# Graph network on one core: one unread 16-bit product of 384 columns before each transposition of edge features

## The chip, the cores and the metric

The kernel runs on one core of a Trainium2 chip. The metric is the device time of one execution in microseconds (us). The core has TensorE (PE; its weight loads are listed as PEld), VectorE (DVE), ScalarE (ACT), GpSimd (POOL) and SyncE (SP), which only issues transfers here. A measurement of this kernel can tell a change of about 0.2% (8 us) from no change.

## What is computed

Four layers of a graph network over 3125 nodes with 128 features and 103125 directed edges (50000 drawn pairs in both directions, and one loop per node), each of the form "normalise, clip at zero, layer, add to x". Cut to what matters here:

```python
h = jnp.maximum(_layernorm(x, axis=-1), 0.0)
# layer 0: a message per edge, summed by source node
msg_input = concatenate([h[dst], edge_attr_64], axis=1)
m = leaky_relu(msg_input @ msg_w1 + msg_b1) @ msg_w2 + msg_b2
aggregated = segment_sum(m, src)
x = x + leaky_relu(concatenate([h, aggregated]) @ upd_w1 + upd_b1) @ upd_w2 + upd_b2
# layer 1: attention with a weight per edge type; layers 2 and 3: sums over the same edges
```

The stage that the change touches makes, for every edge, the row `edge_attr_64 @ msg_w1[128:]` and puts it at the edge's place in a list that is sorted by pairs of node tiles.

## The kernel before

The nodes lie in 25 tiles of 128, so that an edge falls into one of 625 bins (tile of src, tile of dst). A first stage counts the edges of each bin. The second, called the scatter here, is the one that is changed. Later stages go through the sorted rows, build matrices of counts, and do the layers as dense products.

The edges lie 806 to a partition ("columns" of 128 edges). A body of the scatter's loop handles 26 columns in two halves of 13 (`CH`), and there are 31 bodies (62 halves). In one body:

- SP loads the 64 features of the edges of a half into `ef` (L639 to L644) when TensorE has turned the last pair that lay in that half's buffer (`s_te`).
- TensorE goes through 13 pairs of columns (`step`, L838). For a pair q it turns two columns at once (L844, a 32-bit transposition of 128 columns into `pe_t[:, q % 2, 0:P]`), which ACT copies to `eT` (L703); the pair before is then multiplied with `w1bb` (L836, 32 bits, 256 columns, carried out in two passes that the trace lists separately) and ACT copies the result into `rows` (L687). For q equal to 0 and `MEET` (6) the product L836 stands ahead of the transposition. `pe_t` has two banks of 512 words a partition, of which a transposition uses the first 128 words.
- Between the pairs TensorE also works for the half after next: it turns one-hot matrices (L805), spreads the bins over the partitions (L813, 16-bit products of 128 columns) and looks up where a bin begins (L826).
- VectorE works out each edge's place: 13 sums `junkR` (L761), the look-up (L766 to L771), then, for the half after, the one-hots (L731 to L740) and 13 sums `junkW` of the relation's weight (L745), and only then the place as an integer, `posi` (L754).
- POOL sends each column with an indirect transfer to its places in `sorted_rows` in HBM (L885), 26 in a body. Ahead of the first column of a half it waits for `posi` and for the indices, and ahead of the first, fifth and ninth column for `s_cq`, the count of pairs that ACT has copied into `rows` (`NEED`: 2, 4 and 7 pairs in the first half, 9, 11 and 13 in the second).
- ACT fills the index columns of a half (L696, L698) only when the scatters that last read this half of `rows` have landed and VectorE's sums L745 are there.

So the queue that a reader should follow is POOL's: nothing else in the stage reaches `sorted_rows`, and the next stage starts when the last transfer has landed.

Of the kernel before, what the change touches and what calls it, by code (L numbers as in the profile page):

```python
# [22 lines left out]
P = 128  # L23
# [53 lines left out]
def build(nc, x, src, dst, ea, et, w1, b1, w2, b2, u1, c1, u2, c2,  # L77
# [6 lines left out]
    with ExitStack() as top:  # L84
# [102 lines left out]
        with ExitStack() as srt:  # L187
            def sb(name, shape, dt=F32):
                return srt.enter_context(nc.sbuf_tensor(name, shape, dt))
# [10 lines left out]
            identh = sb("identh", [P, P], F16)  # L200
# [365 lines left out]
            with ExitStack() as ctx:  # L566
# [3 lines left out]
                def pb2(name, shape, dt=F32):  # L570
                    return ctx.enter_context(nc.psum_tensor(name, shape, dt))
# [26 lines left out]
                pe_t = pb2("s_pet", [P, 2, BANK])  # L598
# [31 lines left out]
                def prev(i, q):  # L630
                    return (i, q - 1) if q else (i - 1, PAIRS - 1)

                def after(i, h):
                    return (i, 1) if h == 0 else (i + 1, 0)
# [162 lines left out]
                def _(pe):  # L797
                    def turn(i, h, first):
                        n = i * 2 + h
                        pe.wait_ge(s_hv, n + 1)  # L800
                        if not first:
                            pe.wait_ge(s_ot, n)
                        for q in range(4):
                            a, b = 4 * q, min(4 * q + 4, CH)
                            last = nc.tensor.transpose(tq[0:(b - a) * QP, q, :], ohF[:, h, a:b, :].rearrange("p c s -> p (c s)"), identh[:])  # L805
                        last.then_inc(s_tt, 1)

                    def bin_rows(i, h, g, first):
                        n = i * 2 + h
                        if not (first and g < 2):  # L810
                            pe.wait_ge(s_rk, n * 4 + g - 1)
                        for c in range(4 * g, min(4 * g + 4, CH)):
                            last = nc.tensor.matmul(br[:, g % 2, c % 4, :], binh[:, h, c:c + 1].to_broadcast([P, P]), identh[:],  # L813
                                                    start=True, stop=True)
                        last.then_inc(s_br, 1)

                    def lookups(i, h, part, first):
                        n = i * 2 + h
                        if part == 0:
                            pe.wait_ge(s_ot, n + 1)  # L820
                            if not first:
                                pe.wait_ge(s_lc, 3 * n - 2)
                        for q in PARTS[part]:
                            a, b = 4 * q, min(4 * q + 4, CH)
                            k = (b - a) * QP
                            last = nc.tensor.matmul(lk[:, a * NT:b * NT], ohT[0:k, h, q, :],  # L826
                                                    base[0:k, h, q, 0:b - a, :].rearrange("p j d -> p (j d)"), start=True, stop=True)
                        if part == 2:
                            last.then_inc(s_lk, 1)

                    def project(i, q, first):
                        n = i * PAIRS + q
                        pe.wait_ge(s_ce, n + 1)
                        if not (first and q < 2):
                            pe.wait_ge(s_cq, n if q == 0 else n - 1)
                        nc.tensor.matmul(pe_q[:, q % 2, 0:2 * D], eT[:, q % 2, :], w1bb[:], start=True, stop=True).then_inc(s_q, 1)  # L836

                    def step(i, first, final):  # L838
                        for q in range(PAIRS):
                            if q in (0, MEET):  # L840
                                pe.wait_ge(s_row[q // MEET], i * 48 + 48)
                                if not (first and q == 0):
                                    project(*prev(i, q), first)
                            nc.tensor.matmul(pe_t[:, q % 2, 0:P], efv[:, 2 * q * ED:2 * (q + 1) * ED], ident[:], is_transpose=True,  # L844
                                             start=True, stop=True).then_inc(s_te, 1)
                            if q not in (0, MEET):
                                project(*prev(i, q), first)
                            h, r = (0, q) if q < MEET else (1, q - MEET)
                            if not (final and h):
                                to = after(i, h)  # L850
                                if r == 1:
                                    turn(*to, False)
                                if r in (1, 2, 3, 4):
                                    bin_rows(*to, r - 1, False)
                                if r == 5:
                                    for part in range(3):
                                        lookups(*to, part, False)
# [1204 lines left out]
```

## Time and profile before

| | us |
|---|---|
| median of 3 runs | 4012.09 |
| the runs | 4009.74, 4012.09, 4016.07 |
| the profiled execution | 4007.71 |
| its span | 4006.0 |

| engine | busy us | share of the span |
|---|---|---|
| PE | 2767.3 | 69% |
| DVE | 2620.8 | 65% |
| POOL | 1983.2 | 50% |
| ACT | 1608.0 | 40% |

Shares of a whole span are means over stages with different limits. The scatter takes the time from about 278 us to about 1545 us. A row of the timeline gives start, duration, engine, line, operation and tiles, and in square brackets the idle time of the engine before it and what ended that. "issue" is a wait for nothing that the profile shows, "remote" one for a semaphore whose last update the profile can't lay to an instruction. The granted clock is the share of 2.4 GHz that TensorE got; it has two levels, 1.2 and 2.4 GHz.

### The profile page before, as it was taken

What the parts mean: (1) busy time and instruction counts of PE and PEld (TensorE: products, weight loads), DVE (VectorE), ACT (ScalarE), POOL (GpSimd) and SP (SyncE); (2) the same over time, 40 slices, a digit from 0 to 9 for tenths busy, and PEclk for the clock granted to TensorE, in tenths of its full rate; (3) what the DMA queues carried; (4) which work ended last, traced back from release to release, by engine and by line L of the source; (5) the groups of instructions that cost most, each with busy time, mean ns of one, the idle gap of its engine ahead of it and who ended that gap; (6) DMA issues with size and microseconds to landing.
All of it is one profiled execution on the core that took longest, in us unless ns stands there. A gap on an engine that the chain in (4) does not pass through costs nothing. (4 is left out here: it accounts for less than half of the span.)

```text
span 4006.0 us, 89562 instructions
## 1 busy us (share of the span) xinstructions
PE 2767.3 (69%) x19674; PEld 2009.0 (50%) x19675; DVE 2620.8 (65%) x7923; ACT 1608.0 (40%) x4084; POOL 1983.2 (50%) x2354
## 2 busy tenths in 40 slices
PE   2314554455454555888888888888888967769599
PEld 2213333333333334787777877787785222234345
DVE  8724555555555554888888888888886759950501
ACT  1001222222222223776777777776775613320201
POOL 0015666566666666777777777777772000000100
PEclk9955556666666657999999999999999979979797
DMA  9971222221222223777777777777774848848082
GB/s 387 415 291 59 65 65 63 64 62 61 64 64 65 65 64 106 205 203 202 204 204 203 202 206 202 202 205 197 202 206 171 294 173 295 296 151 325 22 325 100
DMA packets 702415, 696.60 MB, mean 174 GB/s; under 512 B 51182, under 2 KB 633536, under 8 KB 692640
## 3 DMA queue, kind: packets, MB, share of 16 engines
q1 hardware_dynamic: 672706, 637.13, 50.5%
q0 software_dynamic: 25792, 54.52, 4.0%
q10 hardware_dynamic: 3870, 4.37, 0.3%
q8 instruction: 24, 0.39, 0.0%
q14 instruction: 23, 0.19, 0.0%
HBM read 340.91 MB, written 354.90 MB: 174 GB/s over the span
## 5 line engine op out<-in xcount | busy, mean ns | idle before, releaser
L885 POOL DMA_INDIRECT sorted_rows<-rows,posi x806 | 779.8, 967 | 577.1 <-issue 246.4
L836 PE MATMUL s_peq<-sb_w1bb,eT 128*128 128x256 f32 x806 | 395.5, 591 | 584.9 <-ACT eT L703 359.6
L1166 DVE SCALAR_TENSOR_TENSOR acc<-acc,keep,pm 128x256 f32<-128x256 f32 x1504 | 717.4, 477 | 76.3 <-DVE acc L1166 36.3
L997 POOL TENSOR_SCALAR ohs_e<-iota,rt 128x128 f32<-128x128 f32 x1128 | 669.6, 608 | 11.4 <-DMA rt<-sorted_rows 11.4
L1093 PE MATMUL pm<-ohw_e,ohs_e 128*128 128x128 f32 x3008 | 662.7, 302 | 0.0
L1006 POOL TENSOR_TENSOR hid<-pre_e,excess 128x512 f32<-128x512 f32 x376 | 498.7, 1326 | 313.5 <-ACT excess L1033 313.5
L836 PEld LDWEIGHTS s_peq<-sb_w1bb,eT 128*128 128x128 f32 x806 | 188.9, 288 | 635.3 <-ACT eT L703 398.7
L1099 PE MATMUL px<-PN,dT 128*128 x4512 | 498.5, 219 | 0.2 <-ACT dT L1040 0.2
L1049 ACT ACTIVATE ohw_e<-ohd_e,rt 128x128 f32<-128x128 bf16 x1504 | 474.6, 386 | 0.0
L1092 PE MATMUL pm<-ohd_e,ohs_e 128*128 128x128 bf16 x1504 | 334.3, 222 | 198.1 <-DVE acc L1166 182.8
L1093 PEld LDWEIGHTS pm<-ohw_e,ohs_e 128*128 128x128 f32 x3008 | 459.7, 193 | 0.0
L703 ACT ACTIVATE eT<-s_pet 128x128 f32<-128x128 f32 x403 | 110.2, 274 | 773.0 <-remote 521.8
L1110 PE MATMUL ps<-hid,ohs_e 128*128 128x129 f32 x3008 | 417.9, 281 | 1.5 <-POOL hid L1006 1.5
L1033 ACT ACTIVATE excess<-pre_e 128x512 f32<-128x512 f32 x376 | 237.0, 630 | 420.3 <-DVE pre_e L1154 420.3
L1099 PEld LDWEIGHTS px<-PN,dT 128*128 128x128 bf16 x4512 | 382.8, 99 | 18.5 <-issue 0.5
L1110 PEld LDWEIGHTS ps<-hid,ohs_e 128*128 128x128 f32 x3008 | 365.5, 191 | 2.1 <-POOL hid L1006 1.9
L1978 POOL TENSOR_TENSOR Z<-Z,Q 128x640 f32<-128x640 f32 x5 | 9.1, 1825 | 712.5 <-DVE Q L1956 712.5
L745 DVE SCALAR_TENSOR_TENSOR junkW<-iotar,typc,relt 128x100 f32<-128x100 f32 x806 | 218.7, 319 | 169.5 <-issue 166.9
L1146 DVE TENSOR_TENSOR ohd_e<-iota,rt 128x512 bf16<-128x512 bf16 x376 | 265.0, 705 | 83.0 <-DMA rt<-sorted_rows 74.2
L1850 PE MATMUL num<-ab,hw 128*128 128x512 f32 (+1 forms) x700 | 274.4, 555 | 18.8 <-DMA ab<-count_matrices 18.8
L1092 PEld LDWEIGHTS pm<-ohd_e,ohs_e 128*128 128x128 bf16 x1504 | 146.2, 97 | 277.8 <-DVE acc L1166 245.3
L761 DVE SCALAR_TENSOR_TENSOR junkR<-s_binrows,binc,later 128x128 f32<-128x128 f32 x806 | 226.5, 345 | 71.5 <-remote 32.6
(299 smaller groups left out, 4469.3 us busy)
## 6 DMA issues: line engine op xcount, KB each, us to landing
count_matrices<-acc SPq DMA_DIRECT2D x1504, 128.0 KB, 2.0
ab<-count_matrices SPq DMA_DIRECT2D x75, 1600.0 KB, 7.8
sorted_rows<-zrow SPq DMA_DIRECT2D x188, 528.0 KB, 9.9
rt<-sorted_rows SPq DMA_DIRECT2D x376, 264.0 KB, 3.0
arb<-count_matrices SPq DMA_DIRECT2D x25, 1664.0 KB, 6.8
arb<-count_matrices SPq DMA_DIRECT2D x25, 1536.0 KB, 6.4
ef<-in_edge_attr_dram SPq DMA_DIRECT2D x60, 364.0 KB
sorted_rows<-rows,posi POOLq DMA_INDIRECT x806
```

Of the source, the lines that this page charges most:

```text
L836: nc.tensor.matmul(pe_q[:, q % 2, 0:2 * D], eT[:, q % 2, :], w1bb[:], start=True, stop=True).then_inc(s_q, 1)
L885: pool.indirect_dma_start(sortd, bass.IndirectOffsetOnAxis(ap=posi[:, h, c:c + 1], axis=0), rows[:, h, c, :], None).then_inc(s_sc[h], 16)
L997: last = nc.gpsimd.tensor_scalar(ohs[:, k, j, :], iota128[:], rt[:, k, j, D + 1:D + 2], None, ALU.is_equal)
L1006: nc.gpsimd.tensor_tensor(hid[:, k % 2, :, 0:D], pre[:, k % 2, :, :], excess[:, k % 2, :, :], ALU.add).then_inc(s_g, 1)
L1049: last = nc.scalar.activation(ohw[:, k, j, :], ohd[:, k, j, :], ACT.Copy, scale=rt[:, k, j, D + 2:D + 3])
L1092: nc.tensor.matmul(pm[:, q, j % 2, 0:P], ohs16[:, kp, j, :], ohd[:, kp, j, :], start=True, stop=True)
L1093: last = nc.tensor.matmul(pm[:, q, j % 2, P:2 * P], ohs[:, kp, j, :], ohw[:, kp, j, :], start=True, stop=True)
L1099: last = nc.tensor.matmul(px[:, kh % 2, j, :], dT[:, kh % 2, j, :], PN[:, ds(dt[j], 1), part, :].squeeze(1), start=(part == 0), stop=(part ...
L1110: last = nc.tensor.matmul(ps[:, k % 2, 0:D + 1], ohs[:, k, j, :], hid[:, k % 2, j, :], start=(j == 0), stop=(j == G - 1))
L1146: nc.vector.tensor_tensor(ohd[:, k, :, :], iota16[:].unsqueeze(1).to_broadcast([P, G, P]), rt[:, k, :, D:D + 1].to_broadcast([P, G, P]), A ...
L1166: nc.vector.scalar_tensor_tensor(acc[:, k % 2, j, :], before, keep[:, at:at + 1] if isinstance(at, int) else keep[:, ds(at, 1)], pm[:, j / ...
L1850: last = nc.tensor.matmul(num[:, c, 0:b - a], hw[:, r, :], ab[:, r, :, :].rearrange("p q d -> p (q d)")[:, a:b], start=first and r == 0, s ...
```

## The change

One matrix product is added ahead of each transposition L844, 403 times in all (13 in a body): the 16-bit identity `identh` as the weights, and the identity again, read three times over, as the moving operand of 384 columns. It writes columns 128 to 511 of the bank of `pe_t` whose first 128 columns the transposition writes. Nobody reads them, and the product signals nothing and waits for nothing of its own. For q equal to 0 and `MEET` it stands behind the product L836 of the pair before, otherwise ahead of it.

```diff
@@ -841,6 +841,8 @@
                                 pe.wait_ge(s_row[q // MEET], i * 48 + 48)
                                 if not (first and q == 0):
                                     project(*prev(i, q), first)
+                            nc.tensor.matmul(pe_t[:, q % 2, P:4 * P].rearrange("p (a b) -> p a b", a=3), identh[:],
+                                             identh[:].unsqueeze(1).to_broadcast([P, 3, P]), start=True, stop=True)
                             nc.tensor.matmul(pe_t[:, q % 2, 0:P], efv[:, 2 * q * ED:2 * (q + 1) * ED], ident[:], is_transpose=True,
                                              start=True, stop=True).then_inc(s_te, 1)
                             if q not in (0, MEET):
```

## Rows read from the trace of the kernel before

**Rows 1.** The page, the span in 40 slices: TensorE's granted clock in tenths

```profile
PEclk9955556666666657999999999999999979979797
```

**Rows 2.** Busy time by stretch: the stage, then two bodies; clock, DMA share, GB/s last

```profile
278.00:1545.00 1267.00, 631.51 (x2647) 433.18 (x2647) 640.48 (x3801) 272.68 (x1019) 779.78 (x806) 0.62 0.20 63
1097.94:1139.41 41.47, 22.31 (x91) 15.85 (x90) 22.11 (x131) 9.04 (x34) 25.22 (x27) 0.58 0.20 63
1139.41:1179.14 39.73, 19.43 (x91) 13.23 (x91) 21.78 (x133) 9.05 (x34) 25.30 (x26) 0.67 0.21 66
```

**Rows 3.** The page's groups: busy, mean ns of one, idle before and its releaser

```profile
L885 POOL DMA_INDIRECT sorted_rows<-rows,posi x806 | 779.8, 967 | 577.1 <-issue 246.4
L745 DVE SCALAR_TENSOR_TENSOR junkW<-iotar,typc,relt 128x100 f32<-128x100 f32 x806 | 218.7, 319 | 169.5 <-issue 166.9
```

**Rows 4.** Waits of POOL, 278 to 1545 us: total, times, longest

```profile
POOL sorted_rows L885 <- ACT rows L687: 238.0, 61, 7.5
```

**Rows 5.** Timeline of POOL: first and last scatter, and the pauses of two bodies

```profile
278.05 1.20 POOL L885 DMA_INDIRECT sorted_rows<-rows,posi  x1 [92.74 <-DMA sorted_rows<-zrow]
...
1097.94 0.95 POOL L885 DMA_INDIRECT sorted_rows<-rows,posi  x1 [3.62 <-ACT rows L687]
...
1108.10 0.96 POOL L885 DMA_INDIRECT sorted_rows<-rows,posi  x1 [0.30 <-issue]
...
1113.82 0.95 POOL L885 DMA_INDIRECT sorted_rows<-rows,posi  x1 [0.30 <-issue]
1119.45 0.95 POOL L885 DMA_INDIRECT sorted_rows<-rows,posi  x1 [4.67 <-ACT rows L687]
...
1134.86 0.96 POOL L885 DMA_INDIRECT sorted_rows<-rows,posi  x1 [0.30 <-issue]
1139.41 0.96 POOL L885 DMA_INDIRECT sorted_rows<-rows,posi  x1 [3.59 <-ACT rows L687]
...
1152.07 0.96 POOL L885 DMA_INDIRECT sorted_rows<-rows,posi  x1 [2.81 <-ACT rows L687]
...
1179.14 0.96 POOL L885 DMA_INDIRECT sorted_rows<-rows,posi  x1 [4.31 <-ACT rows L687]
...
1541.28 0.96 POOL L885 DMA_INDIRECT sorted_rows<-rows,posi  x1 [0.30 <-issue]
```

**Rows 6.** Timeline of PE behind a pause, at the lower clock

```profile
1116.99 1.22 PE L836 MATMUL s_peq<-sb_w1bb,eT 128*128 128x256 f32 x2 [7.36 <-ACT eT L703]
1118.00 0.63 PE L813 MATMUL s_binrows<-identh,binh 128*128 128x128 f16 x4
...
1119.50 0.31 PE L813 MATMUL s_binrows<-identh,binh 128*128 128x128 f16 x1
...
1120.67 1.99 PE L826 MATMUL s_looked<-base,ohT 128*128 128x100 f32 x8
1122.59 0.47 PE L844 MATMUL s_pet<-ident,ef 128*128 128x128 f32 x1
```

**Rows 7.** Timeline of PE, at the higher clock

```profile
1151.47 0.70 PE L836 MATMUL s_peq<-sb_w1bb,eT 128*128 128x256 f32 x2 [0.88 <-ACT eT L703]
1152.91 0.40 PE L813 MATMUL s_binrows<-identh,binh 128*128 128x128 f16 x4 [0.73 <-DVE junkR L761]
...
1153.99 0.23 PE L813 MATMUL s_binrows<-identh,binh 128*128 128x128 f16 x1
```

**Rows 8.** Timeline of ACT: the seventh pair's copy, and the restart at a pause

```profile
1105.83 0.38 ACT L687 ACTIVATE rows<-s_peq 128x256 f32<-128x256 f32 x1 [1.23 <-PE s_peq L836]
1116.66 0.28 ACT L703 ACTIVATE eT<-s_pet 128x128 f32<-128x128 f32 x1 [10.45 <-remote]
...
1118.25 0.39 ACT L687 ACTIVATE rows<-s_peq 128x256 f32<-128x256 f32 x1 [0.37 <-PE s_peq L836]
```

**Rows 9.** Timeline of DVE: the last weight sum of a half and the place

```profile
1136.62 0.32 DVE L745 SCALAR_TENSOR_TENSOR junkW<-iotar,typc,relt 128x100 f32<-128x100 f32 x1 [1.32 <-issue]
...
1138.02 0.17 DVE L754 CAST posi<-posf 128x13 int32<-128x13 f32 x1 [0.60 <-issue]
```

## The prediction

> **What bounds the kernel now.** The slices come first: TensorE's clock stands at five or six tenths from slice 3 to slice 15 and near nine tenths behind them [rows 1]. That stretch is the scatter, the only stage that the change touches; over it TensorE is busy half of the time at a granted clock of 0.62, so a mix of 1.2 and 2.4 GHz [rows 2]. The engine groups then say who is the queue there: POOL issues 806 scatters of 967 ns with 0.30 us between two of them, 1.26 us a column [rows 3, 5]. Twenty-six columns would take 32.8 us, but from the first scatter at 278.05 to the end of the last at 1542.24 a body takes 1264.2 / 31 = 40.78 us. The missing 8 us are pauses: POOL waited 61 times, 238.0 us in all, for ACT's copies of projected pairs, about once a half [rows 4].
>
> The timeline shows what a pause is. POOL's last scatter of a half ends at 1114.77; ACT, idle for 10.45 us although its input was turned long before, goes on at 1116.66, 1.9 us behind that end [rows 5, 8]. At the next pause the last scatter ends at 1135.82, and VectorE, whose sums had crept with gaps of 1.3 us, goes on at 1138.02, 2.2 us behind it [rows 5, 9]. While POOL scatters without a break the other engines all but stop after a few columns; about 2 us after POOL itself pauses they are let go. I call that the release. I can't say from the rows what holds them, only that what ends it is tied to POOL's own stop. So most of a pause is 2 us of release plus what POOL then still needs: in the first half about 1.4 us; in the second the chain copy, product L836 of 1.22 us, copy at 1118.25, then 0.8 us until POOL's scatter at 1119.45 [rows 5, 6, 8].
>
> Not all bodies pause alike. The one from 1097.94 pauses twice at a half's border, 4.67 and 3.59 us (0.3 us of it is the usual gap), and takes 41.47 us. The one from 1139.41 pauses 2.81 us ahead of the ninth column of its first half (at 1152.07), crosses the next border without a pause, pauses 4.31 us at the one after, and takes 39.73 us [rows 2, 5]. An inner pause brings the release earlier and spares one at the border: 1.74 us less. From the mean of 40.78, the share of bodies of the second kind is (41.47 - 40.78) / 1.74 = 0.40.
>
> **The change part by part.** It removes nothing, moves nothing in a queue and adds no wait and no signal; 403 products of 384 columns and their weight loads are put into TensorE's queue. Price of one: four 16-bit products of 128 columns take 0.63 us and one takes 0.31, so each further 128 columns cost 0.107 us at the lower clock; at the higher one (0.40 - 0.23) / 3 = 0.057 [rows 6, 7]. Thus 384 columns cost 0.32 or 0.17 us; the weight load runs beside the product ahead of it, as that of L813 does, which I take as nothing (0.1 us each if that cover fails). In total 403 x 0.32 = 129 us, or 69 us at the higher clock, on an engine that is idle half of the stage.
>
> Where do they lie? TensorE is held for 7.36 us before each restart [rows 6]; what it may run ahead in that time costs nothing. Behind the release it works without a gap at the lower clock, from 1116.99 through look-ups that end at 1122.66 to a transposition at 1122.59 [rows 6]. In this run stand two products ahead of the look-ups (0.64 us), three ahead of the transposition that lets SP load the next features (0.96 us), and a fourth ahead of the seventh pair's L836 (1.28 us, or 0.7 if all were at the higher clock). Who waits for it: VectorE for the look-ups, POOL at its ninth column for the seventh pair. POOL's border pauses themselves start later than any of that and are ended by the release, and the L836 in the chain behind it has no added product in front that could not run earlier.
>
> The ninth column first. In the body from 1097.94 the seventh pair's copy ends at 1106.21, POOL could go 0.8 us later, at 1107.0, and went at 1108.10 [rows 5, 8]. The slack is 1.1 us, the added delay 0.7 to 1.28 us, most of it at the lower clock. So POOL will now often pause ahead of the ninth column where it just didn't before. That is no loss of its own: such a pause makes the release earlier, and the body gets the shorter kind. I take the share of that kind from 0.40 to 0.70, as the delay about equals the slack: 31 x 0.30 x 1.74 = 16 us less. In the remaining 0.30 of bodies I put 0.2 us for a pause too short to release anybody: 2 us more. Sum: 14 us less. Between the ends: share 1.0 gives 31 x 0.6 x 1.74 = 32 us less, and an unchanged share with the whole 1.28 us handed on in each of 62 halves gives 79 us more.
>
> The profiled execution took 4007.71 us (span 4006.0 and 1.7 around it), 4.4 us under the median of 4012.09. The forecast is 3994 for a profiled one, 3998 for the median.
>
> A rule of the Trainium skill speaks for more. What the rows show: the clock is at the lower level right behind each stretch of 7 to 10 us in which TensorE had nothing to do [rows 6], and at the higher one near 1152 after several microseconds of work [rows 7]. "TensorE: Matmul & The Clock Gate", Part 1, says that the throttled clock is the default and that activity releases it. The added products are activity, though none falls into the idle stretches, since they hang in the same queue behind the same waits.
>
> **The rivals.** First, slower: the products lie on a chain that is not forgiven. VectorE's last sum of the half ends at 1136.94 and `posi` follows at 1138.02, the time of the release [rows 9]: a margin of at most 1.1 us, against 0.64 us that the look-ups, and so the thirteen sums, come later, on an engine that at that time creeps with gaps of 1.3 us. From the point at which the delay costs one such step more than the margin, one or two sums are left behind the release, each 0.25 to 0.32 us [rows 3], and POOL's place waits for them: some 0.4 us a half, 62 x 0.4 = 25 us more, 4037. For it speaks that margin and delay are of one size; against it that in the same moment ACT's and TensorE's chain is as long, and covers some of it. Second, no change: the release is tied to POOL's stop, the 16 us of a half's thirteen scatters hide all of TensorE's 2 us more, and the inner pauses come from something other than the pairs' lateness, since the 2.81 us at 1152.07 stand in a body whose pairs were stopped, not slow. Then 4012 within 8. Third, the clock: if TensorE kept 2.4 GHz through the pauses, its L836 behind the release would take 0.70 us in place of 1.22 [rows 6, 7], some 0.45 us of every second pause: 31 x 0.45 = 14 us less, 3998 by another way; with the first term it would be 3984. By the skill's rule this could come; against it stand the idle stretches, which stay. Last, the change may not do what it is made of: if the granted clock of the stage stays at 0.62, TensorE has only got more work, and the first two rivals and the forecast are all that is left; this is how I read it, with 3 in 4.
>
> **How the numbers follow.** The forecast (more inner pauses, 3998) gets 0.38, slower by the delay 0.31, no change 0.23, the clock 0.08. Faster by over 0.2% (8 us, what a measurement can tell) is the forecast and the clock less what of them falls inside 8 us, 0.44; slower 0.32; within 0.24. As both signs hold much, the likeliest case's own range is 3980 to 4004; the range for 8 in 10 goes from 3974 (all bodies of the short kind, and something from the clock) to 4040 (the rival's 25 us and 3 more).
>
> **What would show it.** Right: about as many border pauses fewer as there are pauses ahead of the ninth column more, POOL's total wait for ACT near 225 us in place of 238.0, a clock near 0.65, the stage shorter by 14 us and every stage behind it as long as before. The delay step is right if the look-ups end 6.3 us behind the restart in place of 5.7. Wrong: if `posi` comes later than ACT's copies at the pauses, the first rival holds; if TensorE's first product behind a pause takes 0.70 us, the third. It would also be wrong if the hold on the engines depended on how much TensorE issues: then it would set in earlier, and no row of before can price that.

## The result and the profile after

The change makes the kernel slower. The median went from 4011.09 us (4002.29 to 4018.15, 14 runs) to 4027.32 us (4018.05 to 4035.48, 14 runs), a ratio of 1.0037 with an interval of 1.0025 to 1.0048: 16 us more, where 14 us less were forecast. That lies inside the widest range given (3974 to 4040), on the side of the first two rivals.

The page of the kernel after gives TensorE's clock in 40 slices and the group of POOL's scatters (busy, mean ns of one, idle before them and what ended most of it):

```profile
PEclk9956676666666667999999999999998979979797
L887 POOL DMA_INDIRECT sorted_rows<-rows,posi x806 | 779.2, 967 | 576.0 <-ACT rows L687 242.0
```

Within the stage one slice stands at five tenths, where five did before [rows 1]. The scatters cost what they did [rows 3]. Over the stage, busy time by engine with the granted clock, DMA share and GB/s last:

```profile
278.30:1545.00 1266.70, 700.24 (x3037) 463.71 (x3037) 624.92 (x3801) 277.98 (x1019) 779.15 (x806) 0.66 0.20 63
```

TensorE does 390 of the added products in the records of this stretch and 68.7 us more work [rows 2], at a clock of 0.66 against 0.62. POOL's waits over the stage (total, times, longest):

```profile
POOL sorted_rows L887 <- ACT rows L687: 242.0, 78, 5.6
```

That is hardly more time than before, in 78 waits in place of 61 [rows 4]. The stage of this one execution is not longer than before: 1262.4 us from the first scatter to the end of the last, against 1264.2. This profiled execution is 18.6 us longer all the same, and what is longer is the time behind the last scatter, 2483.9 us against 2463.7. So this pair of traces puts the cost outside the stage that was changed, and profiles of the same two kernels in the next set of runs put 9 us of it into POOL's idle time in the stage (585.0 against 594.2, the summary lines are not shown). Stages that differ from one execution to the next by as much as the effect can't be judged from one trace each; the first experiments are therefore about where the time is.

What such a pause looks like after the change. POOL's timeline, the last two columns ahead of a pause at the ninth column:

```profile
1141.85 0.95 POOL L887 DMA_INDIRECT sorted_rows<-rows,posi  x1 [0.30 <-issue]
1143.11 0.96 POOL L887 DMA_INDIRECT sorted_rows<-rows,posi  x1 [0.31 <-issue]
1149.23 1.01 POOL L887 DMA_INDIRECT sorted_rows<-rows,posi  x1 [5.17 <-ACT rows L687]
```

TensorE at the same time:

```profile
1132.93 0.27 PE L846 MATMUL s_pet<-ident,ef 128*128 128x128 f32 x1
...
1137.32 1.54 PE L826 MATMUL s_looked<-base,ohT 128*128 128x100 f32 x8
1143.14 1.22 PE L836 MATMUL s_peq<-sb_w1bb,eT 128*128 128x256 f32 x2 [4.29 <-issue]
1144.16 0.53 PE L844 MATMUL s_pet<-identh 128*128 128x384 f16 x1
1144.48 0.42 PE L846 MATMUL s_pet<-ident,ef 128*128 128x128 f32 x1
1144.69 0.53 PE L844 MATMUL s_pet<-identh 128*128 128x384 f16 x1
1145.01 0.42 PE L846 MATMUL s_pet<-ident,ef 128*128 128x128 f32 x1
1146.78 1.22 PE L836 MATMUL s_peq<-sb_w1bb,eT 128*128 128x256 f32 x2 [1.35 <-ACT eT L703]
```

And ACT:

```profile
1142.82 0.28 ACT L703 ACTIVATE eT<-s_pet 128x128 f32<-128x128 f32 x1 [4.54 <-remote]
1144.91 0.38 ACT L687 ACTIVATE rows<-s_peq 128x256 f32<-128x256 f32 x1 [1.81 <-PE s_peq L836]
1146.45 0.28 ACT L703 ACTIVATE eT<-s_pet 128x128 f32<-128x128 f32 x1 [1.16 <-PE s_pet L846]
...
1148.04 0.38 ACT L687 ACTIVATE rows<-s_peq 128x256 f32<-128x256 f32 x1 [0.66 <-PE s_peq L836]
```

TensorE stood right behind the look-ups, with the sixth pair's product L836 still to do. The engine that is held, in the sense that it stands though its input is there, is ACT: the sixth pair had been turned by 1133.20, ACT copied it at 1142.82 only, and the product started 0.04 us behind the end of that copy. So it is throughout: in the traces of before and after, whole and cut, each product L836 that follows 3 us or more of idle time of TensorE starts 0.05 to 0.42 us behind the end of a copy to `eT` (the first of a trace excepted, which waits for its features). Where TensorE is called held here or in the forecast, it waits for ACT. POOL stopped at 1144.07 (1143.11 + 0.96). The pair that its ninth column needs had not even been turned when TensorE went on. The release came at 1146.45, 2.4 us behind POOL's stop; then followed a product of 1.22 us, the copy at 1148.04 and 0.8 us until POOL's column at 1149.23. For comparison the pause of before that the forecast took as its pattern, the one that ends at 1152.07 [rows 5]. POOL's last column ahead of it, TensorE's product for the pair that POOL needs, and ACT's copy of it, each from the trace of before:

```profile
1148.24 1.02 POOL L885 DMA_INDIRECT sorted_rows<-rows,posi  x1 [0.30 <-issue]
```

```profile
1146.92 1.22 PE L836 MATMUL s_peq<-sb_w1bb,eT 128*128 128x256 f32 x2 [2.31 <-issue]
```

```profile
1150.87 0.38 ACT L687 ACTIVATE rows<-s_peq 128x256 f32<-128x256 f32 x1 [3.28 <-PE s_peq L836]
```

There the product had ended at 1148.14, ahead of POOL's stop at 1149.26; the release (1.6 us behind the stop) had only the copy to follow it, and the pause was 2.81 us. The pause of after is 2.4 us longer: 1.6 us for the product and what goes with it (2.78 us from the release to POOL's column against 1.20) and 0.8 us because the release itself came later behind the stop.

### The profile page after: what moved, and what is told of

It is laid out like the page before. It is cut to its first block and busy times, and to the rows that moved or that the text cites. A ratio compares the mean times of both kernels' runs of the same rounds, so it can differ in the third digit from the quotient of the medians.

```text
span 4024.6 us, 90368 instructions
## 1 busy us (share of the span) xinstructions
PE 2851.6 (71%) x20077; PEld 2049.8 (51%) x20078; DVE 2612.4 (65%) x7923; ACT 1613.4 (40%) x4084; POOL 1982.2 (49%) x2354
## 5 line engine op out<-in xcount | busy, mean ns | idle before, releaser
L887 POOL DMA_INDIRECT sorted_rows<-rows,posi x806 | 779.2, 967 | 576.0 <-ACT rows L687 242.0
L836 PE MATMUL s_peq<-sb_w1bb,eT 128*128 128x256 f32 x806 | 375.6, 563 | 415.6 <-ACT eT L703 164.9
L836 PEld LDWEIGHTS s_peq<-sb_w1bb,eT 128*128 128x128 f32 x806 | 175.9, 270 | 495.1 <-ACT eT L703 240.0
L761 DVE SCALAR_TENSOR_TENSOR junkR<-s_binrows,binc,later 128x128 f32<-128x128 f32 x806 | 235.8, 345 | 283.2 <-remote 168.3
L1156 DVE TENSOR_TENSOR pre_e<-px,rt 128x512 f32<-128x512 f32 x376 | 258.8, 688 | 15.6 <-PE px L1101 5.0
```

Source lines behind the costliest of these rows:

```text
L887: pool.indirect_dma_start(sortd, bass.IndirectOffsetOnAxis(ap=posi[:, h, c:c + 1], axis=0), rows[:, h, c, :], None).then_inc(s_sc[h], 16)
```

## The experiments

Six chips were used, and the kernel before ran beside the others on each, so a ratio is to the kernel before of its own chip.

### Is it the products or the code behind them?

The kernels before and after once more; one with 39 products ahead of the loops and none in them; one with two products where the change has one.

```diff
                     turn(0, 0, True)
+                    for q in range(39):
+                        nc.tensor.matmul(pe_t[:, q % 2, P:4 * P].rearrange("p (a b) -> p a b", a=3), identh[:],
+                                         identh[:].unsqueeze(1).to_broadcast([P, 3, P]), start=True, stop=True)
```

Expected of the kernel before, again:

> The kernel before, unchanged, for a second trace of it and as a measure of how much stages move by themselves. Every theory: ratio 1.000 within 0.001; first scatter to last scatter 1264 us within 5 us, the stage of edge rows behind it 1467 us within 5 us.

Expected of the kernel after, again:

> The changed kernel once more, for a second trace. Theory A (delay in the scatter: the products lie on the chain that POOL waits for): the scatter from its first to its last transfer is some 15 us longer than in the kernel before. Theory B (the cost lies behind the scatter: in the first trace of the changed kernel the scatter took 1262.4 us against 1264.2, and the stages behind it 18 us more): the scatter is within 5 us, the stages behind it are 10 to 18 us longer again. Ratio 1.0037 by both.

Expected of the 39 products ahead of the loops:

> The 39 products that the program text of the changed kernel has more are put ahead of the scatter's loop, where TensorE is idle while POOL still waits for the clearing of the rows; none is left beside the transpositions. The program is as long as the changed one, so all code behind lies as far back. Theory B in the form that the place of the code costs the time: 4021 to 4030 us. Theory A, and B in any other form: as the kernel before, ratio 1.000 within 0.001.

Expected of two products each:

> The product ahead of each transposition is made two times (806 products of 384 columns). Theory A: the delay doubles, the scatter is 30 us longer than before or more, ratio 1.008 or above. Theory B by place of the code: the program is longer by 78 products, and the time is between that of the kernel before and of the changed one or a little above it, not near the double. If later pauses are forgiven as forecast (the release moves with them), the scatter stays at about 1262 us.

| kernel | median us | ratio to before | interval | clock |
|---|---|---|---|---|
| before again | 4023.32 | 1.0007 | 0.9996 to 1.0017 | 0.834 |
| after again | 4036.23 | 1.0043 | 1.0027 to 1.0059 | 0.851 |
| 39 ahead | 4020.66 | 1.0000 | 0.9987 to 1.0013 | 0.842 |
| two each | 4031.14 | 1.0032 | 1.0016 to 1.0048 | 0.869 |

The cost is there again, in a set of runs of its own, and it needs the products in the loop. The four traces of this chip were expected to show the stage within 5 us of 1264 without the products; it took 1273.0 us (before), 1266.7 (39 ahead), 1281.1 (after) and 1279.4 (two each). Behind the last scatter they took 2477.7, 2480.1, 2485.7 and 2475.7 us, which goes by no order of the products. So here the traces lean towards the scatter, but the kernel before alone moved by more than the 5 us allowed for. Doubling them doesn't double it: the first rival's arithmetic (a delay of so much per product) would have given 1.007 or more. The clock of the whole execution rises to 0.869 and gives nothing back.

### In which stage?

The kernel ends behind the scatter. As before, after, with two products, and with products of 128 columns in place of 384.

```diff
                     for h in range(2):
                         pool.wait_ge(s_sc[h], 16 * CH * BODIES)
+        mid.close()
...
+                sp.dma_start(out[0:(NT - 1) * P, :].rearrange("(t p) d -> p t d", p=P), X[:, 0:NT - 1, :]).then_inc(s_cut, 16)
+                sp.dma_start(out[(NT - 1) * P:N, :], X[0:NR, NT - 1, :]).then_inc(s_cut, 16)
+                sp.wait_ge(s_cut, 32)
+        return
```

and for the short products

```diff
-                            nc.tensor.matmul(pe_t[:, q % 2, P:4 * P].rearrange("p (a b) -> p a b", a=3), identh[:],
-                                             identh[:].unsqueeze(1).to_broadcast([P, 3, P]), start=True, stop=True)
+                            nc.tensor.matmul(pe_t[:, q % 2, P:2 * P], identh[:], identh[:], start=True, stop=True)
```

Expected of the cut kernel before:

> The kernel before, ended behind the scatter: all stages after it (edge rows, the four layers) are left out and x as it stands is written out. For the time of the first two stages by themselves, about 1550 us, over many runs. Its spread tells how much of the whole kernel's spread comes from the scatter.

Of the cut kernel after:

> The changed kernel, ended behind the scatter in the same way. Theory A (the cost lies in the scatter): 13 to 18 us over the cut kernel before. Theory B (it lies behind it): within 4 us of the cut kernel before. The traces so far don't decide: the scatter took 1264, 1273 and 1267 us without the products, 1262 and 1281 with them.

Of two products each, cut:

> As the one with one product ahead of each transposition and ended behind the scatter, with two products each. Theory A with a cost by length: 26 to 36 us over the cut kernel before. If only the kind of pause matters (the pauses move to the fifth and ninth column and stay there): the same as with one product, within 4 us. Theory B: within 4 us of the cut kernel before.

Of 128 columns, cut:

> One product of 128 columns in place of 384 ahead of each transposition, ended behind the scatter: 0.11 us each at the lower clock instead of 0.32, as many instructions. Theory A by length: 4 to 6 us over the cut kernel before. If it is the count of TensorE's instructions that costs: as with 384 columns.

| cut kernel | median us | ratio to the whole kernel before | interval |
|---|---|---|---|
| before | 1559.55 | 0.3878 | 0.3868 to 0.3889 |
| after | 1578.67 | 0.3923 | 0.3912 to 0.3933 |
| two each | 1574.26 | 0.3919 | 0.3906 to 0.3932 |
| 128 columns | 1578.27 | 0.3927 | 0.3914 to 0.3939 |

19 us of 1559.55, all on one chip: a cost as large as that of the whole kernel lies in the scatter. It is as large with products of 128 columns, where a cost by length was to give 4 to 6 us. So it doesn't go by TensorE's time: there a product starts 0.11 us ahead of its transposition at the lower clock, a third of the 0.32 us of the long one. And here the traces show it too, though that of the kernel before is of the fastest of its five executions (1554.85 us), so that it and the trace of after differ by more than the medians. POOL's group in the cut kernel before, over the stage:

```profile
L885 POOL DMA_INDIRECT sorted_rows<-rows,posi x806 | 788.5, 978 | 561.8 <-issue 257.6 <-ACT rows L687 210.2 <-DMA sorted_rows<-zrow 92.8
```

in the cut kernel after:

```profile
L887 POOL DMA_INDIRECT sorted_rows<-rows,posi x806 | 788.3, 978 | 586.6 <-ACT rows L687 247.1 <-issue 246.1 <-DMA sorted_rows<-zrow 92.8
```

with 128 columns:

```profile
L886 POOL DMA_INDIRECT sorted_rows<-rows,posi x806 | 787.2, 977 | 584.8 <-issue 245.8 <-ACT rows L687 245.6 <-DMA sorted_rows<-zrow 92.8
```

and with two products each:

```profile
L889 POOL DMA_INDIRECT sorted_rows<-rows,posi x806 | 784.5, 973 | 585.5 <-issue 256.2 <-ACT rows L687 234.9 <-DMA sorted_rows<-zrow 92.8
```

The 92.8 us lie ahead of the first scatter in all of them; the rest of the idle time grows by 23 to 25 us while the scatters stay as they are. To see which pauses grew I took from each POOL timeline every idle time above 1.3 us between two scatters, and kept those ahead of the ninth column of a half (what the forecast spoke of) apart from all others:

| cut kernel | ninth column: count, us | of these 5 us or longer | others: count, us | all, us |
|---|---|---|---|---|
| before | 30, 74.7 | 3 | 50, 171.1 | 245.9 |
| after | 37, 134.0 | 12 | 43, 137.0 | 271.0 |
| 128 columns | 38, 129.3 | 10 | 43, 139.9 | 269.2 |
| two each | 35, 127.4 | 5 | 48, 143.1 | 270.5 |

So there are more pauses at the ninth column and less time in the others, 34 us less. But the ones at the ninth column cost 59 us more, and most of it isn't their number (7 more) but their length, 3.6 us each in place of 2.5. That is so on this chip. On the chip of the whole kernels above, the same count gives 28 pauses of 107.7 us before (9 of them 5 us or longer) and 38 of 138.2 us after (8 of them), 3.8 and 3.6 us each: there the total at the ninth column rises by 30.5 us and the others fall by 22.6, but the pauses are not longer.

### Does the place in the queue matter?

All 13 products of a body, bunched ahead of two transpositions that TensorE reaches while ACT is held; and one product per half, ahead of the fifth pair of it. Both cut behind the scatter.

```diff
+                            if q in (3, MEET + 3):
+                                for k in range(6 + (q == 3)):
+                                    nc.tensor.matmul(pe_t[:, q % 2, P:4 * P].rearrange("p (a b) -> p a b", a=3), identh[:],
+                                                     identh[:].unsqueeze(1).to_broadcast([P, 3, P]), start=True, stop=True)
```

```diff
+                            if q in (4, MEET + 4):
+                                nc.tensor.matmul(pe_t[:, q % 2, P:4 * P].rearrange("p (a b) -> p a b", a=3), identh[:],
+                                                 identh[:].unsqueeze(1).to_broadcast([P, 3, P]), start=True, stop=True)
```

Expected of the bunched products:

> Ended behind the scatter (all later stages left out). As many added products of 384 columns as in the changed kernel (13 a body), but in two bunches of 7 and 6 ahead of the transposition of the fourth pair of each half, which TensorE runs ahead of the restart, where it then waits 7 us and more. Theory A1 (their time on TensorE's chain between restart and look-ups costs): within 4 us of the cut kernel before (1559.6). Theory A2 (their number in TensorE's queue costs, whatever their length, as 128 columns cost as much as 384): 1574 to 1580 us.

Of one per half:

> Ended behind the scatter. One added product of 384 columns a half (62 in all in place of 403), ahead of the transposition of the fifth pair of the half, that is between restart and look-ups. A1: a sixth to a half of the cost, 3 to 9 us over the cut kernel before. A2: a seventh, 3 us. Theory A3 (the pattern of pauses of the kernel before is a lucky one, and any shift of TensorE's order in time breaks it): 15 to 19 us over it.

Measured: 1546.86 us, 0.3869 (0.3861 to 0.3878), and 1547.45 us, 0.3868 (0.3858 to 0.3878). POOL's group with the products bunched

```profile
L889 POOL DMA_INDIRECT sorted_rows<-rows,posi x806 | 788.1, 978 | 551.0 <-issue 230.9 <-ACT rows L687 226.6 <-DMA sorted_rows<-zrow 92.8
```

and with one per half

```profile
L888 POOL DMA_INDIRECT sorted_rows<-rows,posi x806 | 788.0, 978 | 554.3 <-issue 233.8 <-ACT rows L687 227.2 <-DMA sorted_rows<-zrow 92.8
```

No cut kernel before ran on this chip. Against the ratio 0.3878 of the other chip, neither kernel shows a cost, but whether that ratio may be carried over is not shown: the whole kernel less the cut one leaves 2464.3 us on the chip of the table and 2454.2 us on one that comes below. Taken off the 4002.33 us that the whole kernel before takes here, they leave 1538 or 1548 us for the cut kernel before, and the two kernels would cost between nothing and 9 us. So the runs show less than the 19 us, and up to about half of it isn't ruled out. In the kernel with the products bunched POOL pauses almost only at the borders of the halves (57 pauses of 61, 216.3 of 230.1 us, and a single one at a ninth column).

A last pair of this kind keeps six products of a body (those around and behind the restart of a half), or the other seven:

```diff
+                            if q in (4, 5, 6, 10, 11, 12):
```

```diff
+                            if q in (0, 1, 2, 3, 7, 8, 9):
```

Expected of the first:

> Of the 403 added products only those of pairs 4, 5, 6 and 10, 11, 12 of a body stay (186 in all): in the queue they lie around and behind the restart of a half, before the look-ups and before the seventh (thirteenth) pair's product. The stages behind the scatter are left out and x is written out. Theory A (the place decides: several products between restart and the ninth column's pair make POOL pause there, where a pause is long): nearly the whole cost comes back, a ratio 0.003 to 0.005 above that of the kernel before cut in the same way, many pauses of 3 us ahead of the ninth column. Theory B (what decides is the number of products, wherever they lie in a body): 186 of 403 give about half, 0.002. Theory C (chance of the pattern that the pauses lock into): anything between -0.002 and 0.005, and no relation to the count of inner pauses.

Of the second:

> The complement: the added products of pairs 0 to 3 and 7 to 9 only (217 in all), again with the stages behind the scatter left out and x written out. Theory A: within 0.001 of the cut kernel before, since TensorE works most of them off while it is held or before a border; inner pauses about as many and as long as without any product. Theory B: about half of the cost, 0.002 above the cut kernel before. Theory C: as open as for the other half.

Of the cut kernels before and after beside them:

> The kernel before with the stages behind the scatter left out and x written out, again, as the base for this chip: ratio 0.386 to 0.389 to the whole kernel before.

> All 403 products, the stages behind the scatter left out and x written out, again, on this chip: 0.004 to 0.005 above the cut kernel before by every theory that calls the cost real; within 0.001 if the first comparison of the two was luck of the chip.

This set ran on a chip on which the whole kernel before takes 3785.89 us (3776.76 to 3795.12), and gave 1330.93, 1332.85, 1331.68 and 1331.38 us: in the order of the texts above (ratios 0.3517, 0.3520, 0.3517 and 0.3516, each within 0.0007). All four kernels are alike there, even the one with all 403 products, and the base, expected at 0.386 to 0.389, is far below it. The trace shows what differs; a stretch of POOL's timeline in the cut kernel before on this chip, across a border of a half:

```profile
700.01 0.97 POOL L885 DMA_INDIRECT sorted_rows<-rows,posi  x1 [0.30 <-ACT rows L687]
701.28 0.97 POOL L885 DMA_INDIRECT sorted_rows<-rows,posi  x1 [0.30 <-issue]
...
733.21 0.97 POOL L885 DMA_INDIRECT sorted_rows<-rows,posi  x1 [0.30 <-ACT rows L687]
734.49 0.97 POOL L885 DMA_INDIRECT sorted_rows<-rows,posi  x1 [0.30 <-issue]
```

its group over the stage

```profile
L885 POOL DMA_INDIRECT sorted_rows<-rows,posi x806 | 789.4, 979 | 337.9 <-issue 217.4 <-DMA sorted_rows<-zrow 92.8 <-ACT rows L687 27.7
```

and that of the cut kernel after on the same chip

```profile
L887 POOL DMA_INDIRECT sorted_rows<-rows,posi x806 | 789.6, 980 | 337.9 <-issue 227.7 <-DMA sorted_rows<-zrow 92.8 <-ACT rows L687 17.3
```

One scatter takes as long as on the other chips (979 ns against 978) and stands 0.30 us behind the one before it, as everywhere, but there is no pause: 337.9 - 92.8 = 245.1 us are 805 times 0.30. Over the stage, the cut kernel before and the cut kernel after there:

```profile
278.00:1314.00 1036.00, 533.46 (x2647) 378.53 (x2647) 625.18 (x3801) 269.97 (x1019) 789.43 (x806) 0.69 0.25 77
```

```profile
278.00:1314.00 1036.00, 601.10 (x3037) 420.08 (x3037) 625.43 (x3801) 280.14 (x1019) 789.62 (x806) 0.73 0.25 77
```

VectorE's sums L745, which crept with gaps up to 1.3 us in the kernel before [rows 9], follow one another here in 0.25 us while POOL scatters:

```profile
708.61 0.32 DVE L745 SCALAR_TENSOR_TENSOR junkW<-iotar,typc,relt 128x100 f32<-128x100 f32 x1
...
708.86 0.36 DVE L745 SCALAR_TENSOR_TENSOR junkW<-iotar,typc,relt 128x100 f32<-128x100 f32 x1
```

So the hold is absent on this chip; the 67.6 us that TensorE works more are hidden, and the time is the same. Where POOL doesn't pause the products cost nothing: their cost comes through the pauses, on the chips that have them.

That left the two halves of the change untested where it counts. The first ran once more, on another chip; the second did not:

> The same kernel as cut_chain, once more, because the chip of that call showed no pauses of POOL at all (33.4 us a body with and without products) and so could not tell the theories apart. The stages behind the scatter are left out. On a chip where POOL pauses as in the profile before, a ratio to the whole kernel before of 0.391 to 0.393 by theory A (the products between restart and the ninth column's pair cost the whole +0.004), 0.389 to 0.390 by B (the number counts, half of them here), 0.386 to 0.388 if these six products of a body are not the ones that cost. On a chip without pauses 0.352 again by every theory, since there even all 403 cost nothing (0.3516 against 0.3517).

On a chip with the pauses (whole kernel before 4000.21 us) it took 1546.18 us, 0.3865 (0.3856 to 0.3874). POOL's group:

```profile
L888 POOL DMA_INDIRECT sorted_rows<-rows,posi x806 | 789.2, 979 | 552.8 <-issue 243.0 <-ACT rows L687 216.5 <-DMA sorted_rows<-zrow 92.7
```

That is the ratio of a kernel without a cost, and the whole cost at this place would have given 0.391 to 0.393. Again no cut kernel before ran on this chip: by the same reckoning as above (4000.21 less 2464.3 or 2454.2) that kernel would take 1536 or 1546 us, so half of the cost isn't ruled out. What is shown is that the products behind the restart and ahead of the seventh pair, which my forecast and its first rival both were about, don't bring the whole cost by themselves: three of the four that stand in that stretch are in this kernel (those of q equal to 4, 5 and 6; the fourth, of 7, is not).

### Is the hold tied to POOL's own stop?

POOL waits ahead of the seventh, or the fifth, column of each half until its own columns of that half have landed. Nothing is added to TensorE. Cut behind the scatter, and the first also as a whole kernel.

```diff
                                 pool.sem_inc(s_go, 1)
+                            if c in (6,):
+                                pool.wait_ge(s_sc[h], i * (16 * CH) + 16 * c)
+                                pool.sem_inc(s_go, 1)
                             pool.indirect_dma_start(
```

Expected with the pause ahead of the seventh column:

> Ended behind the scatter. The kernel before with one more wait: ahead of the seventh column of each half POOL waits until its six scatters of that half have landed. If POOL's own unbroken issue is what holds the other engines, and about 2 us of its rest lets them go, the pauses at borders and at the ninth column vanish: a half takes 13 x 1.26 + 2.3 = 18.7 us in place of 20.4, some 100 us less, 1455 to 1490 us. If the pauses come from work of the other engines that is late, the 62 waits of 2.3 us add to them: 1650 to 1700 us.

Ahead of the fifth (`c in (4,)`):

> As the one that waits ahead of the seventh column, but ahead of the fifth, 5 us behind the restart, before the hold as I read it has set in. By the theory of the hold it does less good: what is let go at the fifth column is held again before the half ends: 1540 to 1620 us. If the pauses are other engines' late work: 1650 to 1700 us.

Measured: 1529.45 us, 0.3816 (0.3803 to 0.3829), and 1544.22 us, 0.3856 (0.3844 to 0.3869). The first is 17 us below the bunched products on the same chip, but far above the 1455 to 1490 us that were expected if the pause did away with all others: of the 88 idle times above 1.3 us in its stage only 62 are the added ones. As a whole kernel:

> The whole kernel before, with nothing in TensorE's queue, and POOL waiting ahead of the seventh column of each half until that half's own six scatters have landed. It settles two things. If POOL pauses on this chip as in the profile before, the theory of the hold says that the pause made on purpose is shorter than those it spares: 15 to 25 us less, a ratio of 0.994 to 0.996. At 0.994 the cut kernel with this pause (0.3816) puts the cut kernel before at 0.388 on its chip, and the six, two and bunched products (0.3865, 0.3868, 0.3869) cost nothing; at 0.997 or above it puts it at 0.385 and they would each have cost 0.0015 to 0.002. If the chip is like the one on which nothing is held (3786 us before), each forced pause is a plain loss of about 2.1 us: 62 x 2.1 = 130 us more, 1.034.

3967.51 us (3961.12 to 3974.0), against 3993.28 us of the kernel before on that chip: 0.9938 (0.9920 to 0.9956), 26 us less. This version beats the kernel before on a chip with the pauses. Its price on the chip without them was not measured; the recorded estimate for it is 130 us more. POOL's group in the whole kernel with the pause

```profile
L888 POOL DMA_INDIRECT sorted_rows<-rows,posi x806 | 780.3, 968 | 548.5 <-issue 266.8 <-DMA sorted_rows<-rows,posi 111.5 <-DMA sorted_rows<-zrow 92.8
```

has 577.1 - 548.5 = 28.6 us less idle time than the trace of before ([rows 3] give the 577.1, of another set of runs), though 62 waits were put in. One of them, and what lies around it:

```profile
919.12 0.96 POOL L888 DMA_INDIRECT sorted_rows<-rows,posi  x1 [0.31 <-issue]
920.39 0.96 POOL L888 DMA_INDIRECT sorted_rows<-rows,posi  x1 [0.30 <-issue]
923.49 0.96 POOL L888 DMA_INDIRECT sorted_rows<-rows,posi  x1 [2.14 <-DMA sorted_rows<-rows,posi]
```

It is 2.14 us, about the length after which the others are let go (1.6 to 2.4 us in the rows above). In the two kernels with the pause at the seventh column no idle time of POOL between two scatters reaches 5 us. It also serves as a bridge between chips, if the pause saves the same share on both: 0.3816 for the cut kernel with the pause and 0.9938 for the whole one put the cut kernel before at 0.3816 + 0.0062 = 0.3878, the value measured on its own chip. The intervals of the two terms make it uncertain by 0.0022. Against it 0.3865, 0.3868 and 0.3869 are no cost, and a cost of 0.0044 is out of reach; one of 0.002 is not, and that the share is the same on two chips was not measured.

## Why the prediction was wrong

**What held.** The price of a product: it starts 0.32 us ahead of the next instruction at the lower clock (1144.16 to 1144.48). TensorE's 68.7 us more in the stage look like the lower of the two totals, but they are a net figure: with more of the stage at the higher clock its other work got shorter (the products L836 alone took 366.9 us of the stage in place of 385.5). The delay behind a restart: two products were to put the look-ups 0.64 us later, from 3.68 us behind the restart [rows 6]. TensorE of the kernel after at a restart at the lower clock:

```profile
477.56 1.22 PE L836 MATMUL s_peq<-sb_w1bb,eT 128*128 128x256 f32 x2 [3.67 <-ACT eT L703]
...
479.00 0.52 PE L844 MATMUL s_pet<-identh 128*128 128x384 f16 x1
...
480.49 0.52 PE L844 MATMUL s_pet<-identh 128*128 128x384 f16 x1
...
481.88 0.37 PE L826 MATMUL s_looked<-base,ohT 128*128 128x100 f32 x1
```

That is 4.32 us, 0.64 more. The clock was to be near 0.65 and is 0.66. The third rival fell: the first product behind a pause still takes 1.22 us. The move of the pauses to the ninth column came too: in the whole kernels 38 pauses there in place of 20, and 45 elsewhere in place of 52. The 45 hide something that the forecast didn't have: pauses at the border fell from 42 to 9, and those ahead of the fifth column rose from 4 to 29.

**What failed** is the step "such a pause makes the release earlier, and the body gets the shorter kind", 1.74 us saved per body. It took that from one body of each kind [rows 5]. All bodies but the first and the last, sorted by whether POOL pauses for more than 1.3 us ahead of a ninth column:

| kernel | with such a pause: bodies, mean us | without: bodies, mean us |
|---|---|---|
| before | 16, 41.07 | 13, 41.48 |
| after | 27, 40.99 | 2, 42.60 |
| before again | 20, 41.53 | 9, 41.39 |
| cut before | 25, 40.97 | 4, 41.30 |
| cut after | 26, 41.80 | 3, 41.79 |

In the kernel before the two kinds differ by 0.4 us, and single bodies scatter by 1.2 us, so a saving of 1.74 us was not there to be had. The share was off too: 16 of 29 is 0.55 and not 0.40, and the mean of 40.78 from which the 0.40 was worked out takes in the first body, which lasts 33.1 us without a pause. The inner pause does spare the next border (in 15 of 19 halves of the kernel before), but costs nearly as much itself. The added products did raise the share, to 27 of 29 bodies, more than forecast; where both cut kernels ran on one chip the share hardly moved, and the bodies with an inner pause got 0.8 us longer. Inner pauses come in kinds, and in the two examples above the kinds differ by what TensorE has still to do when POOL stops: 2.8 us where only ACT's copy was missing, 5.2 us where the release was followed by a product and its copy. In the cut kernels the pauses elsewhere shrank by 34 us and those at the ninth column grew by 59: plus 25 us in the two traces, which are themselves 24 us apart, and 19 us in the medians. The 0.2 us that I allowed for "a pause too short to release anybody" was the only loss in the sum. POOL's total wait for ACT was to be 225 us and was 242.0.

**Where TensorE stands when ACT is held.** In each trace I took every idle time of TensorE above 3 us that begins after 312 us (behind POOL's first body) and ends in the product L836, and counted how many of the body's 13 transpositions it had done by then. Six done means one of two places: at the fifth pair's product, ahead of the look-ups, or right behind the look-ups with the sixth pair's product ahead, as at 1143.14 above.

| kernels | waits with six transpositions done | of these behind the look-ups |
|---|---|---|
| whole, no cost: before in two traces, 39 ahead | 1, 2, 2 | 1, 2, 2 |
| whole, with the cost: after in two traces, two each | 9, 11, 14 | 5, 5, 2 |
| cut, no cost seen: before, bunched, one per half, six of 13 | 1, 0, 1, 1 | 1, 0, 1, 1 |
| cut, with the cost: after, two each, 128 columns | 14, 14, 12 | 8, 1, 8 |

Among these 13 traces the count divides the kernels that cost from those that show no cost without an exception. It is a correlation: no run moved this count alone, and with POOL's own pauses it is 4 or 5. The mechanism of the rows at 1143.14 stands behind part of it only. With one product TensorE is found behind the look-ups 5 to 8 times, but with two it nearly always stands ahead of them, 1 or 2 times behind, no more often than in kernels without the cost. In the cut kernel with two products the pauses of 5 us or longer are also fewer (5) and the total is as high. So the pause at 1149.23 is an example of how a pause gets long, and that it accounts for the cost is not shown.

**The rivals.** The first one named the right side and nearly the size (25 us), by a mechanism that didn't happen, so its nearness is luck: it made border pauses longer, through `posi`, and those shrank. In the trace after, POOL's waits on L754 add up to 0.3 us in the stage. The second (hidden) is true on the chip where nobody is held, and is not what the other chips show.

**What stays open.** Why TensorE is caught earlier with all 13 products and rarely with six of them or with all of them bunched (1 and 0 times in the table). It isn't their columns (128 do the same) and not simply their number (26 do the same, 13 bunched bring at most about half). A cut kernel before on the chips of the bunched and the six products would have told whether those cost nothing or half. The seven products that the last kernel left out ran alone only on the chip without pauses. What holds the engines at all stays open too; the rows show that it ends 1.6 to 2.4 us behind POOL's stop, and a chip can be without it.

## What to carry to other kernels

When waits are expected to move, price them from all the bodies of the trace and not from one of each kind; here the two examples differed by 1.74 us and the means of 16 and 13 bodies by 0.4. Inner pauses of 2.8 and of 5.2 us stood at the same line. Ask of a change that only lengthens an idle engine's queue where in its queue that engine will be caught when something stops it. Where a stage's pauses vary between executions, end the kernel behind that stage and compare medians, run the cut kernel before on every chip on which a cut version runs, and look at more than one chip before a pause is taken as part of the kernel.

## What was not expected of the hardware

- One chip of six runs this kernel in 3785.89 us where the others take 3993 to 4024. Most of the difference is the scatter: POOL's idle time in the stage, past the 92.8 us ahead of it, is 245.1 us there and 469.0 us on another (561.8 - 92.8), with scatters of 979 and 978 ns. TensorE's stage clock is 0.69 there.
- A pause of POOL of about 2.1 us, put in 62 times, makes the whole kernel 26 us faster where the engines are held, at a clock of the stage (last but two) that is no higher than before:

```profile
278.00:1520.00 1242.00, 625.16 (x2647) 418.75 (x2647) 620.94 (x3801) 277.72 (x1019) 780.18 (x806) 0.61 0.20 64
```

- Added products raise the granted clock, from 0.62 to 0.66 over the stage with one each, and to 0.869 over the whole execution with two each, against 0.834 of the kernel before on that chip. The time that this should give didn't come: both kernels are slower. "TensorE: Matmul & The Clock Gate" of the Trainium skill, Part 1, says that activity releases the throttled clock; the traces agree as to the clock. In this stage, whose end is set by POOL's waits, it brought no time.
